# Message layers of a graph kernel: first one-hots an octet ahead in two sets, sums in two PSUM banks by turns, one PE signal for each unit

## The chip, the cores and the metric

The kernel runs on 1 core of one Trainium2 chip. Its time is the device time of one launch, in microseconds (us). Before the change the median of three runs is 9792.43 us (9779.41 to 9849.83). TensorE is called PE here, VectorE DVE, ScalarE ACT, GpSimd POOL and SyncE SP, as in the profile.

## What is computed

Four graph networks follow each other on one graph of 4096 nodes with 256 features and 65,536 edges, sorted by target node (dst). Targets are drawn as 4096 u^2, so low nodes have many edges and high ones few. The change touches the first network alone, five message layers:

```python
for l in range(L):                                # L = 5
    h_in = h + vn[batch]
    emsg = relu(h_in[src] + edge_attr @ We[l] + be[l])
    agg = segment_sum(emsg, dst, num_segments=N)  # sums by target node
    t = h_in + agg
    t = relu(t @ W1[l] + b1[l]) @ W2[l] + b2[l]
    t = batch_norm(t)                             # folded into W2 and b2 by the kernel
    if l < L - 1: t = relu(t)
    h = t + h_in
    ...                                           # vn, a vector, for the next layer
```

After it come a weighted sum of neighbours with a linear map, an attention network and three plain convolutions, each of which gathers rows by src and sums them by dst too. A layer norm ends each.

## The kernel before

**Tiling.** Edges stand in tiles of 128, one edge to a partition, 512 tiles in all. Eight tiles are an octet (U = 8), so a layer has 64 octets (NO), worked on in a loop of 16 rounds with four octets written out in each. Nodes stand in 32 blocks of 128. An octet's edges, being sorted, reach into one block or a few; span_row holds for each octet its first block (lo) and their number (cnt). A *unit* is one octet summed into one block: eight matmuls of a one-hot matrix (edge by node of the block, 128x128, f32) with the messages (128x256), collected in a PSUM bank, and then added to the block's rows in AGG by DVE. An octet has one first unit and cnt - 1 further units; a layer has 95 units, of which 31 are further ones. Toward the end of a layer most octets have two blocks.

**An octet in a message layer.** POOL issues eight indirect gathers of node rows (gather_octet, L346) into the ring, which holds four octets. PE encodes the edge attributes (encode, eight bf16 matmuls of L663 into psE). DVE adds psE to the gathered rows (L961). ACT takes the ReLU (L831, signal message). PE sums the unit (L737). If the octet reaches into another block, the block before is complete, and a pipeline for it stands between the units: DVE puts its sum into tin (put_in, L228), PE turns it (turn, L675), ACT copies it to tT (L795), PE makes the hidden layer (hid, L685), ACT takes its ReLU (L787), and, a block later, PE makes the result in two halves (result, L696), DVE adds the bias (scaled, L904) and finishes the block (finish, L933 to L938), ACT stores it as the next layer's table.

**What sets the order.** Each engine has its own program, in the order written, and waits on semaphores. PE: encode of octet h+1 (its first matmul signals octet_free, which lets POOL gather octet h+3), first unit of h, then for each further block: first half of result, further unit, turn, second half of result, hid. DVE: the eight adds of h, then the unit: half the one-hots (four tiles, L264), the add of the unit *before* from PSUM into AGG (L899), the other half; then, for a further block, the bias add, the same three steps, put_in and finish. ACT: eight ReLUs of h, new indices, and the pipeline's steps.

**Around the change.** There is one tile S for one-hots, in two halves, and one PSUM bank for sums, psA; its neighbour psT holds what turn makes. DVE overwrites half g of S when PE has used it in the unit before (onehot_used, +4 for each half), adds when the whole unit is through, and PE starts a unit when the last unit has been added (unit_added) and half the one-hots are there (onehot_ready). The passes after the message layers (weighted_pass, conv_pass) already make first one-hots an octet ahead, in tiles of their own, and signal once for each unit.

## Time and profile before

| | |
|---|---|
| runs, median (lowest, highest) | 9792.43 us (9779.41, 9849.83) |
| span of the profiled execution | 9657.2 us |
| that execution's own time | not given apart from its span; the runs lie 122 us (lowest) to 135 us (median) above the span |
| PE busy | 6002.1 us, 62% of the span |
| POOL busy | 5082.5 us, 53% |
| DVE busy | 3786.7 us, 39% |
| ACT busy | 2061.0 us, 21% |
| mean granted TensorE clock | 0.792 of full speed |
| message layers in the span | from its start to about 4930 us |

The profile is of one execution. A page gives sums by engine and by group of instructions (line, engine, operation, tiles), and for each group the idle time of the engine before it with what ended it. More was asked of the same trace: tables of stretches, tables of who waited for whom, and instructions in order of time. In a row of the timeline stand the start and the length in us, the engine, the line, the operation, the tiles written and read, the count of merged instructions, and in brackets the idle time before with its releaser. "remote" is a releaser that the profile doesn't find among the core's engines, "issue" is idle time with nothing found that was waited for. A matmul of f32 shows as two, so a unit is 16 rows' worth.

### The profile page before, as it was taken

What the parts mean: (1) busy time and instruction counts of PE and PEld (TensorE: products, weight loads), DVE (VectorE), ACT (ScalarE), POOL (GpSimd) and SP (SyncE); (2) the same over time, 40 slices, a digit from 0 to 9 for tenths busy, and PEclk for the clock granted to TensorE, in tenths of its full rate; (3) what the DMA queues carried; (4) which work ended last, traced back from release to release, by engine and by line L of the source; (5) the groups of instructions that cost most, each with busy time, mean ns of one, the idle gap of its engine ahead of it and who ended that gap; (6) DMA issues with size and microseconds to landing.
All of it is one profiled execution on the core that took longest, in us unless ns stands there. A gap on an engine that the chain in (4) does not pass through costs nothing. (4 is left out here: it accounts for less than half of the span.)

```text
span 9657.2 us, 132376 instructions
## 1 busy us (share of the span) xinstructions
PE 6002.1 (62%) x28184; PEld 4644.1 (48%) x28185; DVE 3786.7 (39%) x8268; ACT 2061.0 (21%) x6047; POOL 5082.5 (53%) x5128
## 2 busy tenths in 40 slices
PE   4667666766676667656665674556665566456556
PEld 3456545554565456445543563444453454344344
DVE  4445443444444444444441224445561232222123
ACT  2223222222222222222222323333330000000000
POOL 4545464445444645554456653544316665665666
PEclk8889878887888788778877886777786787777677
DMA  4333332233233323333332224654423322332333
GB/s 124 99 92 95 102 106 86 87 99 103 87 89 101 103 86 91 98 102 92 94 96 83 83 65 142 203 175 164 157 88 92 95 86 82 91 87 77 90 94 88
DMA packets 434108, 984.73 MB, mean 102 GB/s; under 512 B 125952, under 2 KB 210432, under 8 KB 417536
## 3 DMA queue, kind: packets, MB, share of 16 engines
q0 software_dynamic: 245760, 673.51, 24.2%
q1 hardware_dynamic: 130864, 194.89, 6.3%
q10 hardware_dynamic: 57296, 114.45, 3.5%
q14 instruction: 147, 1.20, 0.0%
q8 instruction: 41, 0.67, 0.0%
HBM read 844.97 MB, written 137.49 MB: 102 GB/s over the span
## 5 line engine op out<-in xcount | busy, mean ns | idle before, releaser
L346 POOL DMA_INDIRECT ring<-node_table,idx x4608 | 4559.3, 989 | 3743.2 <-issue 1784.7
L737 PE MATMUL psAT<-ring,S 128*128 128x256 f32 x7600 | 2054.3, 431 | 967.0 <-DVE AGG L899 820.6
L737 PEld LDWEIGHTS psAT<-ring,S 128*128 128x128 f32 x7600 | 1618.5, 219 | 1355.2 <-DVE S L264 704.8
L264 DVE SCALAR_TENSOR_TENSOR S<-iota,block_start,dst_f 128x512 f32<-128x512 f32 x950 | 710.0, 747 | 1294.3 <-remote 891.4
L961 DVE TENSOR_TENSOR ring<-ring,psE 128x256 f32<-128x256 f32 x2560 | 902.9, 415 | 695.5 <-remote 369.5
L831 ACT ACTIVATE ring<-ring 128x256 f32<-128x256 f32 x2560 | 845.0, 408 | 1067.9 <-DVE ring L961 626.6
L1076 PE MATMUL psE<-ring,shared 128*128 128x256 f32 x2304 | 723.7, 461 | 328.9 <-issue 255.0
L1364 POOL DMA_INDIRECT ring<-att_table,idx x512 | 522.3, 1020 | 761.1 <-ACT idx L1568 480.9
L1076 PEld LDWEIGHTS psE<-ring,shared 128*128 128x128 f32 x2304 | 504.2, 229 | 534.3 <-issue 376.5
L663 PE MATMUL psE<-we_stk,stk 128*128 128x256 bf16 x2560 | 429.3, 302 | 396.0 <-DVE ring L961 184.4
L1191 DVE TENSOR_TENSOR AGG<-AGG,psE x288 | 120.8, 419 | 1378.5 <-remote 879.3
L795 ACT COPY tT<-psAT 128x256 f32<-128x256 f32 x160 | 59.5, 372 | 2189.9 <-PE psAT L675 1595.3
L1092 PE MATMUL psE<-ring,stk 128*128 128x256 f32 x1488 | 385.9, 418 | 200.1 <-DVE stk L272 155.9
L663 PEld LDWEIGHTS psE<-we_stk,stk 128*128 128x128 bf16 x2560 | 241.5, 104 | 542.0 <-DVE ring L961 248.0
L685 PE MATMUL psO<-tT,w_sb 128*128 128x128 f32 x2560 | 369.9, 306 | 159.4 <-ACT tT L795 158.3
L1092 PEld LDWEIGHTS psE<-ring,stk 128*128 128x128 f32 x1488 | 312.1, 212 | 275.8 <-issue 226.3
L685 PEld LDWEIGHTS psO<-tT,w_sb 128*128 128x128 f32 x2560 | 351.7, 217 | 193.2 <-ACT tT L795 187.3
L272 DVE SCALAR_TENSOR_TENSOR shared<-iota,block_start,dst_f 128x1024 f32<-128x1024 f32 x192 | 247.3, 1288 | 340.7 <-issue 340.6
L899 DVE TENSOR_TENSOR AGG<-AGG,psAT 128x256 f32 x480 | 200.9, 419 | 436.8 <-remote 245.0
L332 ACT COPY idx<-src_i 128x8 int32 x576 | 109.6, 190 | 1061.7 <-issue 742.1
L1076 PE MATMUL psE<-ring,S 128*128 128x256 f32 x768 | 227.2, 444 | 113.3 <-issue 50.0
L415 PE MATMUL psE<-ring,shared 128*128 128x256 f32 x768 | 218.6, 440 | 102.8 <-ACT ring L483 55.9
(344 smaller groups left out, 6594.3 us busy)
## 6 DMA issues: line engine op xcount, KB each, us to landing
ring<-node_table,idx POOLq DMA_INDIRECT x4608
rows_table<-ring SPq DMA_DIRECT2D x64, 1072.0 KB
ring<-rows_table ACTq DMA_DIRECT2D x64, 1072.0 KB
stk<-stack_table SPq DMA_DIRECT2D x256, 256.0 KB
node_table<-tab ACTq DMA_DIRECT2D x237, 128.0 KB, 1.9
stack_table<-stk SPq DMA_DIRECT2D x64, 256.0 KB
ring<-att_table,idx POOLq DMA_INDIRECT x512
tT<-in_edge_attr SPq DMA_DIRECT2D x68, 64.0 KB
```

Source lines behind the costliest of these rows:

```text
L264: nc.vector.scalar_tensor_tensor(S[:, 4 * g:4 * g + 4, :], iota[:, :].unsqueeze(1).to_broadcast([P, 4, P]), block_start[:, bass.ds(blk, 1) ...
L272: return nc.vector.scalar_tensor_tensor(out, iota[:, :].unsqueeze(1).to_broadcast([P, U, P]), block_start[:, bass.ds(blk, 1)], dst_f[:, ba ...
L346: nc.gpsimd.indirect_dma_start(ring[:, q, 0:gw], None, table, bass.IndirectOffsetOnAxis(ap=idx[:, q:q + 1], axis=0)).then_inc(gathered[q], 16)
L415: ins = nc.tensor.matmul(bank, S_first[ob][:, u, :], ring[:, U * ob + u, 0:D], start=(u == 0), stop=(u == U - 1))
L663: ins = nc.tensor.matmul(psE[:, D * u:D * u + D], stk[:, ob, P * u:P * u + P], we_stk[:, :], start=True, stop=True)
L685: ins = nc.tensor.matmul(psO[:, P * j:P * j + P], w1_sb[:, f, P * j:P * j + P], tT[:, 0, P * f:P * f + P], start=(f == 0), stop=(f == 1))
L737: ins = nc.tensor.matmul(psA[:, 0:D], S[:, u, :], ring[:, U * ob + u, 0:D], start=(u == 0), stop=(u == U - 1))
L831: nc.scalar.activation(ring[:, q, 0:D], ring[:, q, 0:D], ACT.Relu).then_inc(message, 1)
L961: nc.vector.tensor_tensor(ring[:, q, 0:D], ring[:, q, 0:D], psE[:, D * u:D * u + D], ALU.add).then_inc(pre_added, 1)
L1076: ins = nc.tensor.matmul(bank, S_first[ob][:, u, :], ring[:, U * ob + u, 0:D], start=(u == 0), stop=(u == U - 1))
L1092: ins = nc.tensor.matmul(bank, hots[:, u, :], ring[:, U * ob + u, 0:D], start=(u == 0), stop=(u == U - 1))
L1364: nc.gpsimd.indirect_dma_start(ring[:, U * (ob % 2) + u, 0:GW], None, att_table, bass.IndirectOffsetOnAxis(ap=idx[:, q:q + 1], axis=0)).th ...
```

## The change

There are now two sets of first one-hots, used by turns (hot_sets: S and a part of shared), each a whole unit's eight tiles, made by one instruction; DVE makes the set of octet h+1 while it works on h, and that of the first octet before the loop. A further unit's one-hots stand in two other halves (hot_halves: dst_i, free by then, and a part of shared), one signal for both. For an octet's second block they are made ahead of the add, for a third or later block behind it. Sums go by turns to two PSUM banks (two_banks, psA and what was psT), so PE waits for the add of the unit before last, not of the last. PE signals onehot_used once for each unit (+8), not for each half. onehot_ready is gone. turn writes to psO, the bank of hid, and waits for the hidden layer's ReLU. The second half of result now stands ahead of turn. scaled writes to tin's second half. DVE keeps the octet's lo and cnt in registers and reads those of the next octet.

```diff
--- before.py
+++ after.py
...
-        def one_hots(dve, h, blk, c, g):
-            dve.wait_ge(onehot_used, c + 4 * g + 4)
-            nc.vector.scalar_tensor_tensor(
-                S[:, 4 * g:4 * g + 4, :], iota[:, :].unsqueeze(1).to_broadcast([P, 4, P]),
-                block_start[:, bass.ds(blk, 1)],
-                dst_f[:, bass.ds(U * h + 4 * g, 4)].unsqueeze(2).to_broadcast([P, 4, P]), ALU.add, ALU.is_equal
-            ).then_inc(onehot_ready, 4)
...
             Hc, Hn = (H, Y) if l % 2 == 0 else (Y, H)
-            tmp = shared[:, 8 * D:9 * D]
+            tmp = tin[:, 1, :]
+            hot_sets = (S[:, :, :], shared[:, 6 * D:6 * D + U * P].rearrange("p (u e) -> p u e", u=U))
+            hot_halves = [t.rearrange("p (u e) -> p u e", e=P)
+                          for t in (dst_i[:, :].bitcast(F32), shared[:, 6 * D + U * P:6 * D + 3 * U * P // 2])]
+            def two_banks(eng, c):
+                at = nc.s_assert_within((c & U) * (512 // U), 0, 512, skip_runtime_bounds_check_because="0 or 512")
+                return psAT[:, bass.ds(eng.snap(at), D)]
...
                         pe.wait_ge(f_in, n)
                         pe.wait_ge(f_copied, n)
+                        pe.wait_ge(f_relu, n + n)
                         for f in range(2):
-                            ins = nc.tensor.transpose(psT[:, P * f:P * f + P], tin[:, 0, P * f:P * f + P],
+                            ins = nc.tensor.transpose(psO[:, P * f:P * f + P], tin[:, 0, P * f:P * f + P],
                                                       ident[:, :])
...
-                            def unit(first):
+                            def first_unit():
                                 c = pe.snap(npe)
-                                pe.wait_ge(unit_added, c + 5 * U)
+                                bank = two_banks(pe, c)
+                                pe.wait_ge(unit_added, c + 4 * U)
+                                pe.wait_ge(hot_first, (NO + 1) * l + h + 1)
                                 for u in range(U):
-                                    if first:
-                                        pe.wait_ge(message, NT * l + U * h + u + 1)
-                                    if u % 4 == 0:
-                                        pe.wait_ge(onehot_ready, c + u + 4)
-                                    ins = nc.tensor.matmul(psA[:, 0:D], S[:, u, :], ring[:, U * ob + u, 0:D],
+                                    pe.wait_ge(message, NT * l + U * h + u + 1)
+                                    ins = nc.tensor.matmul(bank, hot_sets[ob % 2][:, u, :], ring[:, U * ob + u, 0:D],
                                                            start=(u == 0), stop=(u == U - 1))
-                                    if u % 4 == 3:
-                                        ins.then_inc(onehot_used, 4)
+                                ins.then_inc(onehot_used, U)
                                 pe.reg_add(npe, npe, U)
 
-                            unit(True)
+                            def further_unit():
+                                c = pe.snap(npe)
+                                bank = two_banks(pe, c)
+                                pe.wait_ge(unit_added, c + 4 * U)
+                                pe.reg_add(ng_pe, ng_pe, 1)
+                                pe.wait_ge(hot_further, pe.snap(ng_pe))
+                                for u in range(U):
+                                    ins = nc.tensor.matmul(bank, hot_halves[u // 4][:, u % 4, :],
+                                                           ring[:, U * ob + u, 0:D],
+                                                           start=(u == 0), stop=(u == U - 1))
+                                ins.then_inc(onehot_used, U)
+                                pe.reg_add(npe, npe, U)
+                            first_unit()
                             with pe.If(cnt > 1):
                                 with pe.Fori(1, cnt):
                                     n = pe.snap(nf_pe)
                                     result(n, 0)
-                                    unit(False)
+                                    further_unit()
+                                    result(n, 1)
                                     turn(n)
-                                    result(n, 1)
                                     hid(n)
...
-                        nc.scalar.copy(tT[:, 0, :], psT[:, 0:D]).then_inc(f_copied, 1)
+                        nc.scalar.copy(tT[:, 0, :], psO[:, 0:D]).then_inc(f_copied, 1)
...
+                    nc.vector.memset(psAT[:, :], 0.0)
                     dve.wait_ge(sums_start, l + 1)
+                    dve.drain()
...
-                    def add_sums():
+                    def add_sums(c):
+                        dve.wait_ge(onehot_used, c + 2 * U)
+                        dve.wait_ge(unit_added, c + 5 * U)
                         a = block_of(AGG, last(), AW)
-                        return nc.vector.tensor_tensor(a, a, psA[:, 0:D], ALU.add)
+                        return nc.vector.tensor_tensor(a, a, two_banks(dve, c), ALU.add)
+                    def further_hots(h, b):
+                        for g in range(2):
+                            ins = nc.vector.scalar_tensor_tensor(
+                                hot_halves[g], iota[:, :].unsqueeze(1).to_broadcast([P, 4, P]),
+                                block_start[:, bass.ds(b, 1)],
+                                dst_f[:, bass.ds(U * h + 4 * g, 4)].unsqueeze(2).to_broadcast([P, 4, P]),
+                                ALU.add, ALU.is_equal)
+                        ins.then_inc(hot_further, 1)
...
+                    for reg, value in zip(now_dve[0], span_of(dve, 0)):
+                        dve.reg_mov(reg, value)
+                    hot_unit(hot_sets[0], 0, a_block(dve.snap(now_dve[0][0]))).then_inc(hot_first, 1)
                     with dve.Fori(0, NG) as i:
                         for ob in range(OB):
                             h = OB * i + ob
                             o = NO * l + h
-                            lo, cnt = span_of(dve, h)
+                            lo, cnt = (dve.snap(reg) for reg in now_dve[0])
+                            then = span_of(dve, octet_behind(h))
...
-                            def unit(blk):
+                            c = dve.snap(nd)
+                            add_sums(c - U).then_inc(unit_added, U)
+                            dve.reg_add(nd, nd, U)
+                            hot_unit(hot_sets[(ob + 1) % 2], octet_behind(h), then[0]).then_inc(hot_first, 1)
+                            dve.reg_mov(last_blk, lo)
+                            def further(j):
+                                n = dve.snap(nf_dve)
+                                b = a_block(lo + j)
                                 c = dve.snap(nd)
-                                one_hots(dve, h, blk, c, 0)
-                                dve.wait_ge(onehot_used, c + U)
-                                dve.wait_ge(unit_added, c + 4 * U)
-                                add_sums().then_inc(unit_added, U)
-                                one_hots(dve, h, blk, c, 1)
+                                if isinstance(j, int):
+                                    further_hots(h, b)
+                                    add_sums(c - U).then_inc(unit_added, U)
+                                else:
+                                    add_sums(c - U).then_inc(unit_added, U)
+                                    further_hots(h, b)
                                 dve.reg_add(nd, nd, U)
-                            unit(lo)
-                            dve.reg_mov(last_blk, lo)
+                                scaled(n)
+                                dve.drain()
+                                put_in(n, last())
+                                finish(n, a_block(dve.snap(done_dve[1])), a_block(dve.snap(done_dve[2])))
+                                dve.reg_mov(done_dve[2], done_dve[1])
...
+                                dve.reg_add(nf_dve, nf_dve, 1)
+                                dve.drain()
                             with dve.If(cnt > 1):
-                                with dve.Fori(1, cnt) as j:
-                                    n = dve.snap(nf_dve)
...
-                                    scaled(n)
-                                    unit(b)
...
-                                    dve.drain()
+                                further(1)
+                                with dve.If(cnt > 2):
+                                    with dve.Fori(2, cnt) as j:
+                                        further(j)
+                            for reg, value in zip(now_dve[0], then):
+                                dve.reg_mov(reg, value)
 
                     c = dve.snap(nd)
                     n = dve.snap(nf_dve)
                     scaled(n)
-                    dve.wait_ge(onehot_used, c + U)
-                    dve.wait_ge(unit_added, c + 4 * U)
-                    add_sums()
+                    add_sums(c - U)
...
```

**Order on DVE, octet h's second block (layer 1).** tin, AGG and psV are the block's input tile, the sums and the result's bank; S, dst_i and shared hold one-hots. Before, from the bias add to the copy into tin:

```order
L904 TENSOR_TENSOR shared<-psV,bias_row 128x256 [waits f_result]
L972 ISA
L264 ISA [waits onehot_used]
L264 SCALAR_TENSOR_TENSOR S<-iota,block_start,dst_f 128x512
L975 REGISTER_ALU
L976 REGISTER_ALU [waits onehot_used]
L894 ISA [waits unit_added]
L899 TENSOR_TENSOR AGG<-AGG,psAT 128x256
L264 SCALAR_TENSOR_TENSOR S<-iota,block_start,dst_f 128x512 [waits onehot_used]
L979 REGISTER_ALU
L228 ISA [waits f_turned]
L228 TENSOR_SCALAR tin<-AGG 128x256
```

With the change, the same place, from the first half of the one-hots to the wait ahead of the copy into tin:

```order
L917 SCALAR_TENSOR_TENSOR dst_i<-iota,block_start,dst_f 128x512
L917 ISA
L917 SCALAR_TENSOR_TENSOR shared<-iota,block_start,dst_f 128x512
L910 REGISTER_ALU
L911 REGISTER_ALU [waits onehot_used]
L906 ISA [waits unit_added]
L913 REGISTER_ALU
L913 ISA
L913 TENSOR_TENSOR AGG<-AGG,psAT 128x256
L1015 REGISTER_ALU
L927 TENSOR_TENSOR tin<-psV,bias_row 128x256 [waits f_result]
L227 ISA [waits f_turned]
```

The one-hots (now into dst_i and shared) stand ahead of every wait for onehot_used. One wait for that signal, ahead of the add, is left of three, and the bias add (psV) has moved behind the add.

**Order on DVE, from an octet's last ring add on (layer 1).** Before:

```order
L961 TENSOR_TENSOR ring<-ring,psE 128x256 [waits gathered7]
L972 ISA
L264 REGISTER_ALU [waits onehot_used]
L264 ISA
L264 SCALAR_TENSOR_TENSOR S<-iota,block_start,dst_f 128x512
L975 REGISTER_ALU
L976 REGISTER_ALU [waits onehot_used]
L894 ISA [waits unit_added]
L899 TENSOR_TENSOR AGG<-AGG,psAT 128x256
L264 ISA [waits onehot_used]
L264 SCALAR_TENSOR_TENSOR S<-iota,block_start,dst_f 128x512
```

With the change:

```order
L988 TENSOR_TENSOR ring<-ring,psE 128x256 [waits gathered7]
L998 ISA
L911 REGISTER_ALU [waits onehot_used]
L906 ISA [waits unit_added]
L913 REGISTER_ALU
L913 ISA
L913 TENSOR_TENSOR AGG<-AGG,psAT 128x256
L1000 REGISTER_ALU
L261 REGISTER_ALU
L261 ISA
L261 SCALAR_TENSOR_TENSOR shared<-iota,block_start,dst_f 128x1024
L1027 COMPARE_AND_BRANCH
```

The add now comes first, and the one-hots behind it, 128x1024 in one, are the next octet's.

**Order on PE, a further block (layer 1).** Before, from the end of result's first half to the start of its second:

```order
L696 MATMUL psV<-w_odd,hT 128x256
L729 ISA
L736 REGISTER_ALU [waits unit_added]
L737 MATMUL psAT<-ring,S 128x256 [waits onehot_ready]
L737 MATMUL psAT<-ring,S 128x256 x3
L736 REGISTER_ALU
L737 MATMUL psAT<-ring,S 128x256 [waits onehot_ready]
L737 MATMUL psAT<-ring,S 128x256 x3
L741 REGISTER_ALU
L675 MATMUL psAT<-ident,tin 128x128 [waits f_copied,f_in]
L675 MATMUL psAT<-ident,tin 128x128
L696 MATMUL psV<-w_odd,hT 128x256 [waits f_relu]
```

With the change:

```order
L695 MATMUL psV<-w_odd,hT 128x256
L741 ISA
L745 ISA [waits unit_added]
L748 REGISTER_ALU [waits hot_further]
L748 ISA
L748 MATMUL psAT<-ring,dst_i 128x256 x4
L748 MATMUL psAT<-ring,shared 128x256 x4
L752 REGISTER_ALU
L695 MATMUL psV<-w_odd,hT 128x256 [waits f_relu]
L695 MATMUL psV<-w_odd,hT 128x256
L674 MATMUL psO<-ident,tin 128x128 [waits f_relu,f_copied,f_in]
L674 MATMUL psO<-ident,tin 128x128
```

The further unit waits for hot_further once, its eight matmuls are not parted by a wait, and both halves of result (psV) stand ahead of the transposes, which write psO.

## Rows read from the trace of the kernel before

**Rows 1.** Stretches: length, then busy us (count) of PE, PEld, DVE, ACT, POOL; PEclk; DMA.

```profile
2085.00:2987.00 902.00, 594.59 (x2764) 479.05 (x2765) 389.37 (x939) 215.77 (x717) 472.06 (x488) 0.81 0.33 96
```

**Rows 2.** Timeline of POOL and PE, octets of one block, layer 2.

```profile
2122.46 0.94 POOL L346 DMA_INDIRECT ring<-node_table,idx  x1 [3.89 <-remote]
...
2141.48 0.95 POOL L346 DMA_INDIRECT ring<-node_table,idx  x1 [0.30 <-issue]
...
2141.71 2.59 PE L663 MATMUL psE<-we_stk,stk 128*128 128x256 bf16 x8 [7.46 <-DVE ring L961]
...
2146.21 0.94 POOL L346 DMA_INDIRECT ring<-node_table,idx  x1 [3.78 <-remote]
```

**Rows 3.** Waits of layer 2's loop: engine and line, releaser, us in all, times, longest.

```profile
POOL ring L346 <- PE psE L663: 201.7, 24, 16.5
DVE S L264 <- remote: 200.1, 21, 17.9
PE psAT L737 <- DVE AGG L899: 190.2, 26, 15.3
...
ACT tT L795 <- remote: 158.6, 15, 19.2
```

**Rows 4.** Timeline of a stall between first and second unit, layer 2.

```profile
2523.48 0.94 POOL L346 DMA_INDIRECT ring<-node_table,idx  x1 [12.90 <-PE psE L663]
...
2530.07 3.72 PE L737 MATMUL psAT<-ring,S 128*128 128x256 f32 x16 [2.33 <-issue]
2530.41 0.42 DVE L904 TENSOR_TENSOR shared<-psV,bias_row 128x256 f32<-128x256 f32 x1
...
2542.24 0.95 POOL L346 DMA_INDIRECT ring<-node_table,idx  x1 [0.30 <-issue]
2546.32 0.75 DVE L264 SCALAR_TENSOR_TENSOR S<-iota,block_start,dst_f 128x512 f32<-128x512 f32 x1 [15.49 <-remote]
...
2547.54 5.97 PE L737 MATMUL psAT<-ring,S 128*128 128x256 f32 x16 [12.89 <-DVE AGG L899]
2548.36 0.29 DVE L228 TENSOR_SCALAR tin<-AGG 128x256 f32 x1 [0.29 <-issue]
...
2553.34 0.38 PE L675 MATMUL psAT<-ident,tin 128*128 128x128 f32 x2
...
2554.43 1.95 PE L685 MATMUL psO<-tT,w_sb 128*128 128x128 f32 x16
...
2556.21 1.04 PE L663 MATMUL psE<-we_stk,stk 128*128 128x256 bf16 x8
...
2557.32 0.94 POOL L346 DMA_INDIRECT ring<-node_table,idx  x1 [14.14 <-PE psE L663]
```

**Rows 5.** Timeline of an octet of two blocks late in layer 2.

```profile
2800.74 3.30 PE L685 MATMUL psO<-tT,w_sb 128*128 128x128 f32 x16 [2.90 <-ACT tT L795]
...
2813.11 0.38 PE L675 MATMUL psAT<-ident,tin 128*128 128x128 f32 x2
...
2814.32 0.95 POOL L346 DMA_INDIRECT ring<-node_table,idx  x1 [0.30 <-issue]
...
2816.55 0.37 ACT L795 COPY tT<-psAT 128x256 f32<-128x256 f32 x1 [10.75 <-remote]
...
2816.98 2.55 PE L685 MATMUL psO<-tT,w_sb 128*128 128x128 f32 x16 [2.62 <-ACT tT L795]
```

**Rows 6.** Timeline: first and last of layer 2's eight long idle times after L904.

```profile
2228.44 0.75 DVE L264 SCALAR_TENSOR_TENSOR S<-iota,block_start,dst_f 128x512 f32<-128x512 f32 x1 [17.92 <-remote]
...
2732.17 0.75 DVE L264 SCALAR_TENSOR_TENSOR S<-iota,block_start,dst_f 128x512 f32<-128x512 f32 x1 [17.37 <-remote]
```

**Rows 7.** The page's group of whole one-hots (count, busy us, mean ns, idle before).

```profile
L272 DVE SCALAR_TENSOR_TENSOR shared<-iota,block_start,dst_f 128x1024 f32<-128x1024 f32 x192 | 247.3, 1288 | 340.7 <-issue 340.6
```

**Rows 8.** DMA table of a stretch in the attention stage: packets, MB, share.

```profile
q14 instruction: 47, 0.39, 0.2%
```

**Rows 9.** Waits of layer 2's loop again: the longest "issue" wait.

```profile
DVE AGG L899 <- issue: 26.2, 21, 4.0
```

20 lines of the change are left out of this document (6 added, 14 removed).

## The prediction

> **What bounds the kernel now.** The table of stretches comes first, since the change touches only the five message layers: the loop of layer 2 takes 902.00 us, and in it PE is busy for 594.59, POOL for 472.06 and DVE for 389.37 [rows 1]. No engine is full. So the bound is a chain, and I looked for where it hands over.
>
> The gathers give a floor. Sixteen of them start between 2122.46 and 2141.48 without a pause [rows 2], one every 19.02 / 15 = 1.27 us, so 10.1 us for an octet's eight and 64 x 10.1 = 650 us for a layer, 250 less than it takes. The table of waits says who stops whom in layer 2 [rows 3]: POOL waited 201.7 us, 24 times, for the PE matmul of L663, whose signal frees a ring slot; PE waited 190.2 us for DVE before units; and DVE waited 200.1 us, 21 times, before one-hots (L264) for "remote", a releaser the profile doesn't find.
>
> The timeline says what that releaser is [rows 4]. A unit on PE starts at 2530.07 and by its row has ended 3.72 later, at 2533.79. The next one-hots wait for nothing but that unit's signal (onehot_used), and start at 2546.32, 12.5 us after it. In between PE, DVE and ACT do nothing, and POOL issues one unbroken run of 16 gathers, from 2523.48 to 2543.19. So **signals that PE gives during a run of gathers reach their readers late, when the run is over**. The same shows in a run of eight [rows 5]: the transposes (L675) end at 2813.49, the copy on ACT that waits for them starts at 2816.55, 1.3 us after the last gather issue. And with octets of one block [rows 2]: the encode that frees a slot starts at 2141.71, when the run is at its end, and the next gather is issued only at 2146.21. DVE's and ACT's own signals show no such delay in these rows. That this lateness exists is shown; why the chip does it, the trace doesn't say.
>
> So one cycle reads like this [rows 4]: run of gathers, everything waits for the late signal (E, at 2546.3), then a piece of work, then the encode at 2556.21 lets POOL start again at 2557.32. From E to POOL's start are 11.0 us, in which POOL is idle. What the change can win is in that piece.
>
> **The change part by part.** *Where a stall stands between an octet's first and its second unit.* Now, after E, come half the one-hots, the add, the other half, a unit on a PE that has cooled (5.97 us for 16 pieces, against 3.72 before the stall), transposes at 2553.34, ACT's copy, hidden layer (1.95 us) and encode. After the change the one-hots of a further unit need no signal of PE: their halves are two other tiles, and DVE makes them ahead of the add (L1006 on). They are made in the stall, and with the second bank PE runs the further unit in the stall as well, and then both halves of the last block's result. Behind E stay: the add and the bias add (0.42 each, as L904's row has it), a drain and the copy into tin 0.29 + 0.29, so 1.4 us; transposes 0.38; 0.7 from their end to the hidden layer, in which ACT copies; the hidden layer, which is now the first work of a cooled PE, 3.3 us (the nearest row is the 3.30 us one [rows 5]) in place of 1.95; and the same 1.1 us from encode to the first gather. That is 1.4 + 0.4 + 0.7 + 3.3 + 1.1 = 6.9 us in place of 11.0, **4.1 us less for each such stall**. They can be counted in the timeline as a one-hot that follows the bias add with over 10 us of remote idle: 7, 8, 8, 8 and 9 in the layers 0 to 4, from 2228.44 to 2732.17 in layer 2 [rows 6], 40 in all. 40 x 4.1 = 164 us. The ends: 0 if the next bound is a late signal again, 5.5 us if PE has not cooled (1.95 for the hidden layer again).
>
> *Where the stall stands before an octet's first unit* (about four in a layer). PE runs the first unit in the stall, since its one-hots are an octet old. But DVE then still stands in the add for the last unit, and behind it are now the whole next one-hots (1.29 us [rows 7]) and then two halves of 0.75: the further unit starts some 3.6 us after E. And the run of eight that begins right after E holds the signal of the transposes anyway, as in rows 5, until about 11.4 us after its start. I count nothing, with ends of -1 and +1 us each, 20 x 1 us.
>
> *The dense end of a layer*, octets 50 to 61 in layer 2, 16 us each: PE has work without a gap from encode to transposes, and then waits for the late signal (2.62 us before the hidden layer [rows 5]). The first unit's one-hots do not end any wait there. Now the second half of the result (1.03 us) stands ahead of the transposes; 1.03 us is less than the 3.1 us by which their signal is late, which covers it. Zero; without that cover it costs 12 x 1.03 us in a layer.
>
> *The octets of one block at the start of a layer*: two of them take 2146.21 - 2122.46 = 23.75 us, 3.78 of them POOL's wait [rows 2]. Nothing that the change moves ends this wait, unless the signals come earlier; zero, and a rival below.
>
> *One signal for a unit, not two*: 475 signals fewer. By itself it buys time only if lateness depends on how many signals stand in line. The trace shows single signals 3 to 14 us late, so the count isn't where the time is; I take 0, and the upper end is the second rival. The Trainium skill (TensorE: Matmul & The Clock Gate, The cost: per-tile semaphore tail) says that increments of matmuls serialize, with 26.3 ns for each in its tail model; by an estimate from that page the change would be worth 475 x 0.026 = 12 us, 0.1%. What the rows show is hundreds of times larger and tied to POOL's runs, so here the measurement decides.
>
> *Costs at a layer's start*: one more one-hot of 1.29 us [rows 7], a load of the first octet's span and a memset that is now four times as wide, ahead of the first octet, where nothing covers them: 3 us, of which less than 2 for the last two by the 0.42 us of an op of 256 columns; 3 x 5 = 15 us. The transposes' wait for both ReLU signals and the bank in psO cost nothing: the hidden layer's ReLU is over long before (the same order as now). tmp in tin and the halves in dst_i only change places.
>
> **Sum**: 15 - 164 = -149 us. The profiled execution has a span of 9657.2 us, so 9508 after. Around it lie about 135 us (the median is 9792.43, and that execution's own time isn't given apart); the sum moves the median to 9792 - 149 = **9643 us**, -1.5%.
>
> **The rivals.**
>
> *The late signals rule on as they do* (0.25). The 4.1 us come back as the next wait: POOL starts earlier, and the transposes' signal falls into its run. For it: the idle of ACT before its copy, 158.6 us by remote in layer 2 [rows 3], is such a wait already. Against: at E no run is on in rows 4, and the transposes come 2 us behind it. Time: 9792 + 15 = about 9807, down to 9752 if a third of the gain is left.
>
> *Signals come through* (0.14). With half of the unit signals gone, those for a free slot and for encode, next in PE's order, arrive inside the run; POOL then goes on without the pauses. For it: of several signals in a run some arrive in time and only the later ones don't. Against: the late ones are late up to the run's end, not by a fixed time each. If half of POOL's 201.7 us a layer went, it would be 5 x 100 = 500 us: about 9300 us.
>
> *Slower: the DVE's loop outgrows its instruction store* (0.07). The body of the message loop grows by a third to a half, as the order of instructions shows (rows 407 to 598 of layer 1 before, 507 to 790 after), because the work on a further block now stands twice. In the message loops of now no instructions are loaded: the DMA table of 2150 to 2950 lists no instruction queue. In the attention stage, with the longest loops, it does, 47 packets between 6200 and 6800 [rows 8]. The point from which it decides is whether a round of the loop has to load again. Its price lies between 0 (covered by a stall) and 4.0 us, the longest wait of L899's adds with no releaser but issue [rows 9]: 16 rounds x 5 layers x 4.0 = 320 us, so with the gain 9963, or 10127 without it. The Trainium skill (Runtime: NRT & Kernel Launch, Instruction fetch mechanics) has the rule behind it: a taken branch to a target outside the two pages of instructions that are held forces a load before execution goes on, which speaks against this change. The trace agrees for the attention stage only.
>
> *The forecast* has 0.54.
>
> **How the numbers follow.** About 1% is what a measurement of this kernel can tell from no change: 9694 and 9890. The forecast's own range is 9570 to 9740 (1.3 to 5.5 us for each stall; the zeros' ends lie within it); about nine tenths of it lie below 9694. With the second rival that gives 0.54 x 0.88 + 0.14 = 0.62 for faster, less a little for the case that I count stalls which aren't on the chain: 0.59. The first rival is within 1%, as is the rest of the forecast: 0.32. The slower side is the third rival, and longer runs that I do not foresee, 0.09. The range reaches down into the second rival and up over the first: 9450 to 9820.
>
> **What would show it.** Right: in the profile after, remote idle before further one-hots is gone and stands before the add (L913) instead; the further unit starts in the stall; from E to POOL's next start are 6 to 8 us; a whole layer loop takes about 870 us. POOL's wait for L661 falls by some 35 us a layer. Wrong: the loop stays at 900 (first rival); runs of 24 gathers and more, and a loop under 820 (second); an instruction queue inside the loop (third). The forecast is wrong if PE's signals turn out late for a reason other than POOL's runs.

## The result, and the profile after

In paired runs on one chip the change takes **9847.81 us** (median of 20 runs, 9798.48 to 9892.71) and the kernel before 9803.86 us (20 runs, 9754.14 to 9855.27): a ratio of 1.0043, 95% interval 1.0027 to 1.0060. It is slower by 0.4%, and inside 1%. Forecast were 9643 us and a range up to 9820. So the range missed it, though "within 1%" had a chance of 0.32.

The kernel before doesn't take the same time in every comparison: its medians in this one and the four below are 9804, 9847, 9775, 9820 and 9629 us, and the second and the last are from the same chip. So every figure is a ratio to the kernel before, run beside it on the same chip, and spans of two profiles don't compare to 1%. An execution's time is 1.8 us above its span (9813.75 and 9812.0 us in the profile after), so the profile of before, with its span of 9657.2 us, is of an execution faster than all 20 of the kernel before here.

What the trace of the change shows, first as the table of stretches has layer 2's loop (length; busy us and count of PE, PEld, DVE, ACT, POOL; PEclk; DMA):

```profile
2157.00:3072.00 915.00, 590.46 (x2752) 467.30 (x2753) 380.24 (x875) 214.29 (x716) 472.32 (x488) 0.82 0.32 94
```

915 us against 902 [rows 1], with the same work of PE and POOL (PE 590.46 us and POOL 472.32; before, 594.59 and 472.06). The 13 us by themselves say little: the passes behind the message layers, which the change doesn't touch, are 38 us longer in this trace too (from the last unit's last matmul to the end, 9812.0 - 5044.3 against 9657.2 - 4927.2). What can be read is that the loop didn't fall to about 870 us, and where the waits stand. The waits of that loop (us in all, times, longest) answer to those of before [rows 3]:

```profile
DVE AGG L913 <- remote: 262.4, 42, 15.6
POOL ring L335 <- PE psE L661: 261.9, 30, 19.1
```

DVE stood before its one-hots for 200.1 us by remote; now it stands before the add of the sums for 262.4, 42 times in place of 21. POOL's wait for the encode was to fall by some 35 us and rose by 60.

One stall of the kind that carried the forecast, from the timeline (start, us, engine, line, operation, idle before):

```profile
2568.76 0.94 POOL L335 DMA_INDIRECT ring<-node_table,idx  x1 [7.86 <-PE psE L661]
...
2572.85 3.65 PE L735 MATMUL psAT<-ring,S 128*128 128x256 f32 x16
...
2575.65 0.75 DVE L917 SCALAR_TENSOR_TENSOR shared<-iota,block_start,dst_f 128x512 f32<-128x512 f32 x1
...
2587.53 0.95 POOL L335 DMA_INDIRECT ring<-node_table,idx  x1 [0.30 <-issue]
2591.96 0.42 DVE L913 TENSOR_TENSOR AGG<-AGG,psAT  x1 [15.56 <-remote]
2592.30 0.42 DVE L927 TENSOR_TENSOR tin<-psV,bias_row 128x256 f32<-128x256 f32 x1
...
2592.85 2.07 PE L695 MATMUL psV<-w_sb,hT 128*128 128x256 f32 x4 [16.34 <-DVE tin L927]
...
2594.71 3.51 PE L748 MATMUL psAT<-ring,dst_i 128*128 128x256 f32 x8
...
2600.65 0.38 PE L674 MATMUL psO<-ident,tin 128*128 128x128 f32 x2
...
2601.50 2.05 PE L684 MATMUL psO<-tT,w_sb 128*128 128x128 f32 x16 [0.46 <-ACT tT L806]
...
2603.39 1.04 PE L661 MATMUL psE<-we_stk,stk 128*128 128x256 bf16 x8
...
2604.49 0.94 POOL L335 DMA_INDIRECT ring<-node_table,idx  x1 [16.02 <-PE psE L661]
```

Read it against [rows 4]. The first part came as forecast: the further halves (L917, the last at 2575.65) are made inside the stall, and the idle time has moved to the add, 15.56 us. But then PE does nothing from the end of its first unit (2572.85 + 3.65) to 2592.85, where it starts the first half of the result (L695), released by "DVE tin L927". That is the bias add, which DVE runs **behind** the add. PE takes its instructions in order, so the further unit (L748, 2594.71) runs behind E too, and the chain from E is: bias add, result, further unit, result, transposes, ACT's copy, hidden layer, encode at 2603.39, POOL at 2604.49. From E to POOL's start are 2604.49 - 2591.96 = 12.5 us, against 11.0 before and 6.9 forecast. In the kernel before PE did run the first half of the result in the stall, right behind its unit:

```profile
2533.62 1.03 PE L696 MATMUL psV<-w_sb,hT 128*128 128x256 f32 x4
```

The page has two more lines that answer to [rows 3] and [rows 8]: the adds over all layers, and the queue that loads instructions (packets, MB, share), whose line in the page of before read 147.

```profile
q14 instruction: 467, 3.83, 0.1%
...
L913 DVE TENSOR_TENSOR AGG<-AGG,psAT x480 | 202.1, 421 | 1740.1 <-remote 1169.1
```

By stretches of the change's trace, in the loop of layer 1 and in the loop of layer 2:

```profile
q14 instruction: 79, 0.65, 0.2%
```

```profile
q14 instruction: 3, 0.02, 0.0%
```

So the third rival came true as well. Layer 2 is the exception: the stretches of the layers 0, 3 and 4 (140 to 1080, 3148 to 4070, 4140 to 5050) list 77, 79 and 89 such packets, though all run about the same loop. The kernel before has 1 to 3 in each of its five loops. The stall above is of layer 2, so loads have no part in it.

### The profile page after: what moved, and what is told of

Its sections match the earlier page's. It is cut to its first block and busy times, and to the rows that moved or that the text cites. A ratio compares the mean times of both kernels' runs of the same rounds, so it can differ in the third digit from the quotient of the medians.

```text
span 9812.0 us, 133030 instructions
## 1 busy us (share of the span) xinstructions
PE 6075.8 (62%) x28184; PEld 4640.1 (47%) x28185; DVE 3748.0 (38%) x7953; ACT 2068.9 (21%) x6047; POOL 5128.9 (52%) x5128
## 5 line engine op out<-in xcount | busy, mean ns | idle before, releaser
L1111 PE MATMUL psE<-ring,shared 128*128 128x256 f32 x2304 | 717.5, 458 | 323.5 <-issue 251.8
L913 DVE TENSOR_TENSOR AGG<-AGG,psAT x480 | 202.1, 421 | 1740.1 <-remote 1169.1
L735 PE MATMUL psAT<-ring,S 128*128 128x256 f32 x2560 | 726.4, 442 | 160.3 <-issue 117.6
L735 PE MATMUL psAT<-ring,shared 128*128 128x256 f32 x2560 | 682.3, 424 | 87.2 <-issue 56.2
L735 PEld LDWEIGHTS psAT<-ring,S 128*128 128x128 f32 x2560 | 552.2, 223 | 309.0 <-issue 222.4
L735 PEld LDWEIGHTS psAT<-ring,shared 128*128 128x128 f32 x2560 | 532.8, 215 | 207.4 <-issue 124.6
L261 DVE SCALAR_TENSOR_TENSOR shared<-iota,block_start,dst_f 128x1024 f32<-128x1024 f32 x352 | 454.1, 1290 | 358.7 <-issue 358.6
L806 ACT COPY tT<-psO 128x256 f32<-128x256 f32 x160 | 59.5, 372 | 2210.5 <-PE psO L674 2120.5
L695 PE MATMUL psV<-w_sb,hT 128*128 128x256 f32 x792 | 237.1, 427 | 412.7 <-DVE tin L927 321.9
L695 PEld LDWEIGHTS psV<-w_sb,hT 128*128 128x128 f32 x792 | 154.8, 207 | 470.8 <-issue 445.5
```

The lines of the kernel that those rows point to most:

```text
L261: return nc.vector.scalar_tensor_tensor(out, iota[:, :].unsqueeze(1).to_broadcast([P, U, P]), block_start[:, bass.ds(blk, 1)], dst_f[:, ba ...
L695: ins = nc.tensor.matmul(psV[:, 0:D], hT[:, 0, P * j:P * j + P], w2[:, j, :], start=(j == 0), stop=(j == 3))
L735: ins = nc.tensor.matmul(bank, hot_sets[ob % 2][:, u, :], ring[:, U * ob + u, 0:D], start=(u == 0), stop=(u == U - 1))
L913: return nc.vector.tensor_tensor(a, a, two_banks(dve, c), ALU.add)
L1111: ins = nc.tensor.matmul(bank, S_first[ob][:, u, :], ring[:, U * ob + u, 0:D], start=(u == 0), stop=(u == U - 1))
```

## The experiments

Fifteen kernels ran, in four groups on three chips (groups 1 and 4 on the same one); each ratio is to the kernel before, run beside it.

### Group 1: the change's two faults, each taken away

**e1_bias_first**: the bias add goes ahead of the add of the sums, in both copies of the further block's code.

```diff
                                     further_hots(h, b)
+                                    scaled(n)
                                     add_sums(c - U).then_inc(unit_added, U)
                                 ...
                                 dve.reg_add(nd, nd, U)
-                                scaled(n)
```

> The changed kernel with one edit: in a further block DVE does the bias add (scaled) ahead of the add of the unit before, as the kernel before does, and not behind it. Theory A (the bias add, moved behind an add that waits for a late PE signal, holds PE in the first half of result, so the further unit no longer fits into the stall): the further unit runs inside the stall, from the stall's end to POOL's next start are some 7 us in place of 12.9, so 40 stalls x 5.5 = 220 us less than the changed kernel, about 9630 us, ratio to before 0.982. Theory B (the loss comes from instruction loads in the DVE's longer loop, which stay here): not over 20 us away from the changed kernel, ratio to before 1.002 to 1.006. Theory C (late PE signals give the gain back elsewhere): ratio 0.995 to 1.005 although the further unit moves into the stall.

Measured: 9723.63 us, ratio 0.9873 (0.9843 to 0.9904), about three quarters of the 220 us that were expected against the change. A stall of its trace, the same kind:

```profile
2589.36 0.42 DVE L927 TENSOR_TENSOR tin<-psV,bias_row 128x256 f32<-128x256 f32 x1
...
2603.72 0.42 DVE L913 TENSOR_TENSOR AGG<-AGG,psAT  x1 [13.94 <-remote]
...
2604.61 1.91 PE L695 MATMUL psV<-w_sb,hT 128*128 128x256 f32 x4
...
2607.41 2.21 PE L684 MATMUL psO<-tT,w_sb 128*128 128x128 f32 x16 [0.46 <-ACT tT L806]
...
2609.46 1.17 PE L661 MATMUL psE<-we_stk,stk 128*128 128x256 bf16 x8
...
2610.57 1.96 POOL L335 DMA_INDIRECT ring<-node_table,idx  x1 [10.30 <-PE psE L661]
```

From E (2603.72) to POOL (2610.57) are **6.9 us**, the forecast's figure. That it is met to a tenth is luck: the second half of the result (L695, 1.91 us) still runs behind E, so that the transposes start 2.6 us after E in place of 1.4, and the hidden layer is over after 2.1 us, where the encode starts, in place of 3.3. PE's waits for the bias add in layer 1's loop, in the change and then in e1_bias_first:

```profile
PE psV L695 <- DVE tin L927: 154.1, 25, 16.5
```

```profile
PE psV L695 <- DVE tin L927: 16.3, 6, 6.9
```

So the order of two DVE instructions of 0.42 us is worth 1.7% (1.0043 to 0.9873, in two comparisons), and turned the sign. The loads stayed in this kernel (542 packets on its page, against 467), so they aren't what turned it.

**e2_one_body**: the further block's code once, as in the kernel before, with the halves ahead of the add; the bias add stays behind the add. A register holds the count at which the halves' tiles are free.

```diff
-                                further(1)
-                                with dve.If(cnt > 2):
-                                    with dve.Fori(2, cnt) as j:
-                                        further(j)
+                                with dve.Fori(1, cnt) as j:
+                                    further(j)
 ...
+                                dve.wait_ge(onehot_used, dve.snap(hots_free))
                                 further_hots(h, b)
                                 add_sums(c - U).then_inc(unit_added, U)
+                                dve.reg_mov(hots_free, c + 2 * U)
```

> The changed kernel with the work on a further block written once, not twice: the one-hots are made ahead of the add for every block, behind a wait for the last further unit's signal against a register; the bias add stays behind the add. The loop in DVE's program gets shorter by about a third. Theory B (instruction loads cost the time): no instruction packets inside the message loops, and the four layers that have them now get shorter by 7 us (layer 1) to 27 us (layer 0), some 45 to 60 us in all, ratio to before 0.998 to 1.000. Theory A (the bias add's place alone matters): instruction packets gone but time within 15 us of the changed kernel, ratio 1.003 to 1.006.

Measured: 9857.21 us, 1.0015 (0.9992 to 1.0037). **e3_both**: both edits.

> Both edits: bias add ahead of the add, and the further block's work written once. Theories A and B together: 220 + 50 us less than the changed kernel, about 9580 us, ratio to before 0.977. If only A holds: as the run with the bias add first, 0.982. If only B holds: as the run with one body, 0.999. Theory C: 0.99 to 1.00.

Measured: **9635.99 us, 0.9786 (0.9756 to 0.9816)**, faster than both kernels. The page of either lists 147 packets of instructions again, as before. The shorter code alone gives 0.3% (1.0043 to 1.0015, two comparisons whose intervals overlap, so hardly told from nothing), and 0.9% once the bias add is ahead (0.9873 to 0.9786, one comparison). Perhaps the loads fall into a stall that is there anyway while the bias add is late; no run here shows that.

**e4_two_signals**: the change with two PE signals for a unit (4 + 4) in place of one.

> The changed kernel with one edit: PE signals onehot_used twice in each unit (+4 after four matmuls and +4 after eight), not once. Theory A and B (the number of signals is not where the time is): within 15 us of the changed kernel, ratio to before 1.003 to 1.006. Rival (lateness depends on how many signals stand in line, so one signal for each unit gained something which hides a larger loss): slower than the changed kernel by 50 us or more, ratio over 1.009, with encode's and the free slot's signals later in the runs of gathers.

Measured: 9895.25 us, 1.0050 (1.0029 to 1.0071): nothing told from the change's 1.0043.

### What still stalls in e3_both

A cycle of its layer 2, from the timeline:

```profile
2502.20 0.94 POOL L336 DMA_INDIRECT ring<-node_table,idx  x1 [9.51 <-PE psE L662]
...
2512.78 0.42 DVE L929 TENSOR_TENSOR tin<-psV,bias_row 128x256 f32<-128x256 f32 x1
...
2513.33 1.13 PE L696 MATMUL psV<-w_sb,hT 128*128 128x256 f32 x4 [1.43 <-issue]
...
2516.15 1.99 PE L749 MATMUL psAT<-ring,dst_i 128*128 128x256 f32 x8 [1.69 <-issue]
...
2517.98 0.38 PE L749 MATMUL psAT<-ring,shared 128*128 128x256 f32 x1
...
2519.57 0.38 PE L749 MATMUL psAT<-ring,shared 128*128 128x256 f32 x1 [1.21 <-issue]
...
2521.47 0.94 POOL L336 DMA_INDIRECT ring<-node_table,idx  x1 [0.30 <-issue]
...
2522.39 0.59 PE L749 MATMUL psAT<-ring,shared 128*128 128x256 f32 x1 [2.45 <-issue]
...
2523.79 0.58 PE L749 MATMUL psAT<-ring,shared 128*128 128x256 f32 x1 [0.81 <-issue]
...
2525.20 1.87 PE L749 MATMUL psAT<-ring,shared 128*128 128x256 f32 x4 [0.83 <-issue]
...
2525.78 0.42 DVE L915 TENSOR_TENSOR AGG<-AGG,psAT  x1 [12.59 <-remote]
...
2532.22 1.04 PE L662 MATMUL psE<-we_stk,stk 128*128 128x256 bf16 x8
...
2533.33 1.34 POOL L336 DMA_INDIRECT ring<-node_table,idx  x1 [10.92 <-PE psE L662]
```

The bias add no longer waits, and PE goes on with the result and the further unit at 2516.15. But the unit's second half comes one matmul at a time, from 2517.98 to 2523.79, starts 1.4 to 2.8 us apart (in the longest a record may be missing: the weight load of one stands at 2520.99), with "issue" before them. By the program's order they wait for no semaphore, and the DMA table of 2512 to 2526 lists no queue that loads instructions. The last gather of the run is issued by 2522.41, and at 2525.20 four follow at once. The stall of e1_bias_first shows the same (single matmuls at 2600.32, 2601.75 and then three at 2603.19). So it is not only that readers learn late of PE's signals: PE itself is held. And the length of all of it follows POOL's run: E comes 2525.78 - 2502.20 = 23.6 us after the first of 16 gathers here, 23.2 in the change (2591.96 - 2568.76), 22.8 in the kernel before [rows 4]. Half of that, 11.6 us, for eight gathers would be over 1.4 us for each, while POOL issues one every 1.25. That is an estimate from three stalls. The idea to test: signals of PE come through late while gathers stand in line, the line grows by a run of gathers, and it is the line that must be broken.

### Group 2: pauses for POOL

**p1_pause2**, **p2_pause4**: e3_both with two or four memsets of one column behind each gather in the message layers, and a wait for their signal ahead of the next octet. **p3_before_pause2** is the kernel before with two. **p4_between** has sixteen behind each octet of eight gathers in place of these:

```diff
+            if k < L:
+                pool.wait_ge(idled, NO * k + OB * i + 1 + ob)
             pool.sem_inc(idx_seen, 1)
             for q in range(U * ob, U * ob + U):
                 ...gather...
+            for n in range(16 if k < L else 0):
+                ins = nc.gpsimd.memset(idle[:, n:n + 1], 0.0)
+            if k < L:
+                ins.then_inc(idled, 1)
```

> e3_both with two memsets of one column on POOL behind each gather of the message layers (one more wait and one signal per octet on POOL keep them in order), about 0.1 us each by the profile's start-up memsets (99 to 119 ns), so gathers would be issued every 1.45 us or so in place of 1.25. The theory (signals of PE get through only between gathers whose processing takes 1.41 us each, so a run of 16 issued every 1.25 us keeps them back until it is over): with the issue no faster than the processing the backlog is gone, PE's signals come as they are made, the further unit's matmuls aren't held, and an iteration of 16 gathers needs 16 x 1.45 = 23.2 us plus what is left of the stall, against 27.6 us in e3_both: 0 to 4.4 us less in each of 160 iterations, 8930 to 9640 us. Rival 1, the lateness is a fixed delay of signals and has nothing to do with the backlog: the stall stays whole (7.6 us) and 3.2 us come on top in each iteration, about 10150 us. Rival 2, POOL's stall takes the slower issue up, the time of e3_both (9636) within 1%.

Measured: 9578.67 us, 0.9805 (0.9782 to 0.9829), like e3_both. The expectation had its dose wrong: gathers still come every 1.25 us in its timeline, since two memsets fit into the 0.3 us between gathers (2500.86 to 2501.00, and the next gather at 2501.16). Only the wait between octets is new in it, so it tells nothing between the theory and its rivals.

> As p1_pause2 with four memsets behind each gather, issue every 1.65 us or so. The theory: nothing is late, and POOL's own 16 x 1.65 = 26.4 us per iteration are the floor: the time of e3_both (27.6 us an iteration) or up to 2% less. Rival 1: 27.6 + 6.4 us an iteration, about 10660 us. Rival 2: as e3_both within 1%.

Measured: 9329.26 us, 0.9543 (0.9516 to 0.9571). That is 2.5% less than e3_both, a little more than the theory allowed, but not by its dose: gathers came every 1.30 us, not 1.65. Between octets POOL waits for its memsets' own signal besides (1.64 us before the gather at 2502.60). How much of the gain is this break between octets, as in p4_between, and how much the memsets between gathers, isn't told apart.

> The kernel before with the two memsets of p1_pause2 behind each gather. If its stall too is made of signals held behind the backlog of gathers, its iteration falls from 28.2 us (902.6 / 32) towards 23.2 to 26 us, 9150 to 9700 us, without anything of the change; then the change was aimed at a symptom. Rival 1: 28.2 + 3.2 us, about 10360 us. Rival 2: no change within 1%.

Measured: 9742.74 us, 0.9968 (0.9951 to 0.9984): rival 2.

> e3_both with sixteen memsets behind each octet of eight gathers in place of some behind each gather: about 1.6 us (16 x 0.1) of pause per eight gathers, which are issued every 1.25 us. The theory: eight gathers have fallen 8 x 0.16 = 1.3 us behind by then, so the pause lets the backlog empty in the middle of a run of 16, and signals that waited come there; between p1_pause2 and e3_both. If the pause must stand between single gathers, it is slower than p1_pause2 by over 1%. Rival 1 (fixed delay): +3.2 us an iteration, about 10150 us.

Measured: **9250.68 us, 0.9483 (0.9448 to 0.9519)**, the opposite of the expected order: the pause between octets beats those between gathers. Rival 1 (a fixed delay) has no room for a gain of 3% on e3_both, and falls. The adds of the sums wait for remote 257.5 us in the whole run, against 1120.1 in e3_both and 1169.1 in the change, and the sixteen memsets take 0.55 us:

```profile
L924 DVE TENSOR_TENSOR AGG<-AGG,psAT x480 | 201.2, 419 | 893.7 <-PE psAT L745 345.5 <-remote 257.5 <-issue 235.1
...
L344 POOL MEMSET idle<- 128x1 bf16 x5120 | 176.4, 122 | 0.1
```

### Group 3: the pause without the change

**p5_before_between** is the kernel **before** with p4_between's pause, **p6_after_between** the change as it was with it.

> The kernel before with p4_between's pause (sixteen memsets behind each octet and a wait for their signal ahead of the next; the next octet's first gather started 12.4 us after the last one's in p4_between, against 10.0 without a wait). If the runs of 16 gathers are what made the signals late in the kernel before as well, it gains what e3_both gained from the same pause (9636 to 9251, 4.2%): about 9400 us. If the gain needs the further unit ahead and the second set (the change's own parts), it stays within 1% of before, or slower, as p3_before_pause2 did (0.997).

Measured: **9163.31 us, 0.9323 (0.9287 to 0.9359)**, a gain of 6.8% where the expectation had 4.2%. So the gain needs nothing of the change.

> The change as it was measured, with p4_between's pause. Its own faults stay (the bias add behind the add of the sums, instruction fetches in four of five layers, together 212 us between the change and e3_both). Theory: with signals on time the bias add no longer waits behind a late add, so that fault costs little, and only the fetches are left: 9250 to 9350 us, and faster than p5_before_between by over 1%. Rival: the order fault costs as much as before, 9400 to 9470 us, about p5_before_between.

Measured: 9429.44 us, 0.9600 (0.9565 to 0.9634). The time is in the rival's range, and the theory's (faster than p5_before_between) fell: with the pause the change gains 4.0%, the kernel before 6.8%. But the rival's reason, that the faults cost as much as before, isn't borne out: between the change and its mended version lie 1.2% with the pause (0.9600 to 0.9483, two chips) and 2.6% without it (1.0043 to 0.9786).

Two octets of p5_before_between:

```profile
2519.96 1.34 POOL L350 DMA_INDIRECT ring<-node_table,idx  x1 [1.97 <-ACT idx L334]
...
2524.77 0.38 PE L684 MATMUL psAT<-ident,tin 128*128 128x128 f32 x2
...
2525.19 0.37 ACT L804 COPY tT<-psAT 128x256 f32<-128x256 f32 x1 [4.38 <-PE psAT L684]
...
2528.64 3.72 PE L746 MATMUL psAT<-ring,S 128*128 128x256 f32 x16
...
2529.34 0.94 POOL L350 DMA_INDIRECT ring<-node_table,idx  x1 [0.30 <-issue]
2530.28 0.55 POOL L354 MEMSET idle<- 128x1 bf16 x16
...
2532.30 0.75 DVE L266 SCALAR_TENSOR_TENSOR S<-iota,block_start,dst_f 128x512 f32<-128x512 f32 x1 [2.89 <-remote]
2532.57 1.29 POOL L350 DMA_INDIRECT ring<-node_table,idx  x1 [1.75 <-ACT idx L334]
```

Eight gathers, the last at 2529.34; the memsets end at 2530.83; the one-hots that wait for PE's signal start at 2532.30, 12.3 us after the run's start, and POOL starts the next eight at 2532.57. Their signal is that of the first four matmuls of the unit at 2528.64, which are over at about 2530.5 (an estimate: half of its row), so the signal is 1.8 us late, where those of the stalls above are 12 to 15 us late. And early in the run a signal is not late at all: the transposes end at 2525.15, 5.2 us after the run's start, and ACT's copy starts at 2525.19. So signals are late near a run's end still, but the run is now eight gathers long, and POOL's next one begins **after** they are through, not before.

The pause is longer than its memsets. From their end to the next gather, in which POOL waits for their own signal, pass another 1.74 us here, and 1.9 us in the median of this trace: with the 0.55 us, octets start 12.4 us apart in place of 10.0. A stretch in the middle of its message layers, by the table of stretches:

```profile
2000.00:2800.00 800.00, 623.60 (x2891) 491.71 (x2889) 409.58 (x967) 240.46 (x722) 523.38 (x1485) 0.87 0.38 111
```

PE does 2891 matmuls in 800 us, against 2764 in 902 [rows 1], it is busy 78% of the time against 66%, and the granted clock is 0.87 against 0.81. Most octets start 12.4 to 12.7 us apart (64 x 12.5 = 800 us for a layer's octets), so POOL's own rhythm is the bound now, and what the change moves is worth nothing any more.

It even costs: e3_both with this pause (0.9483) is behind p5_before_between (0.9323). The traces show one place of it. In the last octets of layer 2 p4_between's runs start 15.0 to 16.3 us apart (2616.54, 2632.53, 2647.58, 2663.88), where p5_before_between keeps 12.4 to 12.8. The transposes, now behind both halves of the result and the further unit, end at 2642.13, 9.6 us into the run, and ACT's copy starts 2.0 us late, at 2644.16; in the cycle of p5_before_between above they are through at 5.2 us. That is the dense end of the layer, which the prediction put at zero. How much of the 1.7% is this, no run separates.

**p7_wait_only** has one memset per octet in place of sixteen, **p8_between48** forty-eight, both on e3_both.

> p4_between with one memset per octet in place of sixteen: what is left is the wait for that memset's signal between octets, with 0.1 us of pause in place of 0.55 us (p4_between's sixteen are 0.55 us busy). If POOL's own signal is held until its run of eight is through (11.3 us for eight gathers of 1.41 us), the octets are apart by that alone, and the time is p4_between's within 1% (9160 to 9345 us). If the pause's length matters (a window in which two or three signals follow one another), it lies between p1_pause2 and p4_between, 9350 to 9580 us.

Measured: 9562.41 us, 0.9741 (0.9705 to 0.9777), and the adds wait as they did:

```profile
L924 DVE TENSOR_TENSOR AGG<-AGG,psAT x480 | 201.6, 420 | 1698.9 <-remote 1025.0 <-PE psAT L745 316.8 <-issue 257.3
```

> p4_between with 48 memsets per octet: 32 more at 0.034 us (0.55 us for sixteen) are 1.1 us more of pause, 320 octets. If the window's length still limits, it is faster than p4_between by 1% or more; if POOL is the bound now, it is slower by up to 320 x 1.1 = 352 us, about 9600 us; equal within 1% if the two balance.

Measured: 9462.52 us, 0.9631 (0.9588 to 0.9674), so the longer pause costs 1.5%, as when POOL is the bound (from the last gather of an octet to the first of the next are 3.3 us in its trace, 2.3 in p4_between's, both medians of 1200 to 2800 us). The wait for POOL's own signal isn't enough, and of the three lengths tried on e3_both (1, 16 and 48 memsets) 0.55 us of memsets is the best.

### Group 4: what was left open

**q2_between8**: the kernel before with eight memsets per octet.

> p5_before_between with eight memsets per octet in place of sixteen, about 0.27 us less pause. If the window is long enough already, POOL's octets come 0.27 us sooner, 320 x 0.27 = 86 us less at most, about 9080 us. If the window must hold the chain of signals that frees the octet after next, the stall comes back in part: between p5_before_between and p3_before_pause2, 9300 to 9700 us.

Measured: 9494.98 us, 0.9866 (0.9841 to 0.9891). Its timeline has what eight memsets less do:

```profile
2494.10 0.94 POOL L350 DMA_INDIRECT ring<-node_table,idx  x1 [0.90 <-POOL idle L354]
...
2502.85 0.95 POOL L350 DMA_INDIRECT ring<-node_table,idx  x1 [0.30 <-issue]
...
2506.03 5.51 PE L746 MATMUL psAT<-ring,S 128*128 128x256 f32 x16 [13.89 <-issue]
...
2515.36 0.95 POOL L350 DMA_INDIRECT ring<-node_table,idx  x1 [11.25 <-PE psE L672]
```

The memsets take 0.32 us in place of 0.55, but here their signal is also back after 0.90 us in place of 1.7 to 2.0, so the octet at 2494.10 starts 10.9 us after the last one (at 2483.19), and its run is on when PE's signals would come. Why the signal is back sooner isn't shown; of the octets of this trace about two in five start so, the others later. PE's next unit runs only at 2506.03, 11.9 us after the run's start, after 13.89 us of "issue", and POOL waits 11.25 us for the encode. In p5_before_between the signals that free the next work are through 12.3 us after a run's start, and the next run begins behind them; here it begins 1.4 us sooner than that, and the stall of a run of 16 is back.

**q1_one_signal**: the kernel before with one signal for a unit, the part that the prediction priced at nothing.

```diff
-                                    if u % 4 == 3:
-                                        ins.then_inc(onehot_used, 4)
+                                ins.then_inc(onehot_used, U)
```

> The kernel before with one PE signal per unit in the message layers in place of one per four matmuls, nothing else. The prediction priced this part of the change at nothing. If it is nothing, the time is before's within 1%. If held signals get through one per gather of 1.41 us, one signal less per unit brings the next unit's one-hots 1.4 us sooner in each of the stalls, at most 160 x 1.4 = 220 us less (2.3%); if the first signal of a unit gave the one-hots a head start, up to 1% slower.

Measured: 9587.56 us against 9628.63, 0.9946 (0.9916 to 0.9977). A gain of 0.5%, with an interval of 0.2 to 0.8%: neither nothing nor the expectation's 2.3%. The change with two signals (e4_two_signals) can't be told from the change itself, so the effect is small, and no run shows it in the change.

**q3_all_passes**: p5_before_between with the pause in the four other passes that gather by the same function.

> p5_before_between with the same pause in the four other passes that gather by the same function (576 - 320 = 256 octets' worth of rows in 4 passes of 64). If PE's signals are held there as well and a later engine waits for them, each of 256 octets that now runs in a longer row gains; the adds of AGG there wait 926 to 952 us for remote in e3_both, so up to 5% less, about 8700 to 9000 us. If these passes are bound by POOL's gathers without stalls, each octet costs its pause, 12.5 - 10.0 = 2.5 us, up to 256 x 2.5 = 640 us more, about 9800 us.

Measured: 8986.61 us against 9628.63, 0.9337 (0.9315 to 0.9358), the ratio of p5_before_between. The time looks like the expectation's faster case only because the kernel before was faster in this comparison; the ratio says that the pause in the four passes neither gains nor costs 1%. Its group of adds of the later passes:

```profile
L1198 DVE TENSOR_TENSOR AGG<-AGG,psE x288 | 120.8, 419 | 1374.0 <-PE psE L1083 1365.2 <-PE psE L1099 4.8 <-issue 4.0
```

The later passes' adds (L1198) wait 1374.0 us, as in the kernel before (1378.5, of which 879.3 for remote). Remote has gone from the first place: the profile finds PE's matmuls (L1083) as the releaser. That fits signals that were late there too and are no longer, but their readers wait as long as before and the ratio is the same, so it isn't what sets these passes' time.

## Why the prediction was wrong

**The bound was read rightly, in the main.** "Signals that PE gives during a run of gathers reach their readers late, when the run is over" holds for the stalls shown of the kernel before, the change, e1_bias_first and e3_both. It doesn't hold for a signal given early in a run (in p5_before_between one given 5.2 us after the run's start is read 0.04 us later). p4_between and p5_before_between show from the other side that this is what the layers wait for.

**The step that failed** is the list of what stays behind E: "Behind E stay: the add and the bias add (0.42 each...)", and before it "PE runs the further unit in the stall as well, and then both halves of the last block's result". The two sentences contradict each other, and I didn't see it. The result's first half needs the bank that the bias add frees, and stands ahead of the further unit in PE's order; the bias add stood behind the add that waits for E. So nothing of PE's part moved into the stall. The prediction also says of that stall, "In between PE, DVE and ACT do nothing", and overlooked the row that would have warned: PE's result at 2533.62, which in the kernel before runs there because the bias add (2530.41) does. I priced the bias add by its duration, 0.42 us, and not by who waits for it. The 4.1 us saved for each stall were 1.5 us lost in the stall shown, and e1_bias_first, which mends only this, has 6.9 us from E to POOL and a ratio of 0.9873: with that order the forecast's size is nearly met (-1.5% forecast, -1.3% measured), though in part by luck. Its 6.9 us are made of other terms, with the result's second half (1.91 us) behind E and the hidden layer shorter than the 3.3 us, and its time still holds the instruction loads, whose removal gave another 0.9%.

**The third rival** (0.07) was real and under-rated. q14 lists 79 packets in layer 1's loop, where the kernel before has one; taking the second copy of the code away took them away, and was worth 0.9% with the bias add ahead. That is 9723.63 - 9635.99 = 88 us, against a price of up to 320. It didn't decide the sign alone. The Trainium skill (Runtime: NRT & Kernel Launch, Instruction fetch mechanics) has a load whenever a taken branch leaves the held instructions. The trace agrees in four of the five layers; layer 2, with 3 packets for about the same code, shows that the length alone doesn't tell.

**The first rival** (0.25, about 9807) came nearest, with 1.0043 measured, but by another mechanism than it named: it was PE's order that put the work behind E, and not POOL's earlier start.

**The second rival** (0.14, about 9300: signals come through) has no support as it was put: fewer signals give 0.5% at most (q1_one_signal). Signals come through when POOL pauses, and that p2_pause4 and p4_between take about the time it gave (9329 and 9251 us) is no point for it: they got there by another edit.

**The zeros.** One signal for a unit was 0 to -0.5% and not the cause. The dense end, the one-block octets and the stalls before a first unit were not tried one by one; e3_both's whole is -2.1% against -1.5% forecast for all, so they hold no large loss there. With the pause the dense end isn't zero, as p4_between shows. "Around it lie about 135 us" between span and median was wrong: an execution's time is 1.8 us above its span (9657.99 and 9656.2 us in e3_both). What I took for time around the span was executions that differ. And by its own terms (1.3 us for each of 40 stalls, and 15 us of costs) the forecast's range should have ended at 9755, not at 9740.

**The larger miss** was to look for work to move into the stall, and not to ask what would shorten the run that makes it. The evidence stood in the rows: in the stall shown everything stands until the run of 16 is over [rows 4].

## What to carry to other kernels

When work is moved into a stall, walk each engine's own order from the first moved instruction on, and for each one ask what it waits for and where that is now queued; a 0.42 us instruction behind a late wait costs the whole wait of those it feeds. And before filling a stall, ask what ends it: here a pause between octets of gathers, 0.55 us of memsets and a wait for their signal, a few lines on the engine that issues them, was worth 6.8%, more than three times what the best version of the change gives.

## What the runs showed of the hardware that wasn't expected

- While a row of indirect gathers is under way on POOL, PE's signals reach other engines late, and it matters when in the row they are given. Given 5.2 us after the start of a row of eight, one was read 0.04 us later (p5_before_between, 2525.15 to 2525.19). In rows of 16, units that ended 7.7 to 10.3 us after the start were read at 22.8 to 23.6 us, 12.5 to 15.5 us late (2533.79 to 2546.32 in the kernel before, 2576.50 to 2591.96 in the change), some 3 us after the last gather's issue. Near the end of a row of eight the lateness is about 2 us. The rows read show no such delay of DVE's and ACT's signals. Why is open; that the gathers' descriptors are the line in which they stand is an idea that no run here tests.
- PE itself is held in such a row: matmuls without waits start singly, 1.4 to 2.8 us apart (e3_both), where 16 rows of a unit otherwise take 3.6 to 3.7 us.
- How sharply the pause's length counts: sixteen memsets (0.55 us) are worth 6.8% on the kernel before, eight (0.32 us) 1.3%; on e3_both sixteen are worth 3.1% (0.9786 to 0.9483, two chips), one 0.5%. The wait for the memsets' own signal comes on top: 1.9 us (median) in p5_before_between, 0.9 us in about two of five octets of q2_between8. Why it is shorter there isn't shown.
- Two memsets of one column behind a gather are free: they fit into the 0.3 us between two gathers (p1_pause2, gathers still 1.25 us apart).
- Whether a loop loads instructions isn't told by its length: 79 packets in one layer's loop of the change, 3 in the next one's, for about the same body.
